# A third scatter accumulator in a mixture-of-experts block: rotated, loaded early, and summed half on VectorE and half in PSUM

## The reference, cut to what matters

```python
x = x + conv(layernorm_over_channels(x), W)       # W: product of 32 reflections, 128 x 128
t = tokens(x)                                     # 4096 tokens of 128 channels, float32
h = softmax(layernorm(t) @ W_router + b_router)   # 32 experts
G, idx = top_k(h.T, 128)                          # each expert picks 128 tokens
up = silu(tokens[idx] @ W_up + b_up)              # 128 -> 341
eo = G * (up @ W_down + b_down)                   # 341 -> 128
y = zeros(4096, 128).at[idx].add(eo)              # a token may be picked by several experts
out = t + y                                       # back to NCHW
```

## Time and profile before

| | us |
|---|---|
| median of 3 runs | 192.45 (191.24 to 192.54) |
| the profiled execution | 192.84 |
| its span, first to last instruction | 191.0 |
| busy: PE, POOL, DVE, ACT | 130.8, 110.7, 83.3, 80.6 |

### The profile page before, as it was taken

How to read it: one execution, slowest core, us unless ns; L and a number is a source line. 1 busy time by engine, 2 the same in 40 slices (tenths; PEclk the granted TensorE clock), 3 DMA queues, 4 the chain that set the end, 5 groups by cost and what they waited for, 6 DMA issues and landing times.

```text
span 191.0 us, 2379 instructions
## 1 busy us (share of the span) xinstructions
PE 130.8 (68%) x670; PEld 86.7 (45%) x673; DVE 83.3 (44%) x374; ACT 80.6 (42%) x290; POOL 110.7 (58%) x119
## 2 busy tenths in 40 slices
PE   0999983432421644479999999998399999500892
PEld 0556972321101412247666787668234444200892
DVE  1464898985578489800112222128912200000550
ACT  3167799554798277854553335540000000000162
POOL 2017658998632037777777788775878878730000
PEclk9999999995555555555999999999969999975588
DMA  4999999999956243222222233341332333378987
GB/s 89 299 329 319 289 294 228 226 407 293 247 169 195 81 184 105 72 69 69 63 63 66 69 44 28 31 40 14 29 28 27 31 33 36 27 160 304 389 261 234
DMA packets 33662, 28.37 MB, mean 149 GB/s; under 512 B 6832, under 2 KB 27376, under 8 KB 33520
## 3 DMA queue, kind: packets, MB, share of 16 engines
q1 hardware_dynamic: 26785, 21.70, 39.0%
q0 software_dynamic: 5424, 4.39, 15.9%
q10 hardware_dynamic: 1440, 2.13, 3.4%
HBM read 17.53 MB, written 10.68 MB: 148 GB/s over the span
## 4 chain that ended last, share of the span: by engine, by line
PE 38%; POOL 20%; DVE 14%; DMA 12%; issue 11%; ACT 4%; SPq 0%; POOLq 0%
POOL acc L503 7%; PE PT L1128 7%; PE PZ L1142 7%; DMA acc<-X,idx 6%; PE PM L1128 6%; POOL rs L464 4%; DMA x<-acc 3%; PE PM L1142 3%; PE PZ L1169 3%; POOL rs L457 3%; PE PT L975 3%; POOL act L470 2%; DMA k<-in_const_f 2%; PE PT L1117 2%; DVE junk L913 2%
## 5 line engine op out<-in xcount | busy, mean ns | idle before, releaser
L503 POOL DMA_INDIRECT acc<-X,idx x27 | 45.6, 1690 | 13.5 <-issue 8.2
L494 POOL DMA_INDIRECT xg<-token_rows,idx x32 | 30.6, 955 | 20.4 <-DVE idx L910 11.9
L632 ACT ACTIVATE X<-PZ 128x512 f32<-128x512 f32 x4 | 2.4, 597 | 52.6 <-PE PZ L1169 52.6
L951 DVE TENSOR_SCALAR X<-PZ,xg 128x128 f32<-128x128 f32 x22 | 7.6, 349 | 27.9 <-PE PZ L1142 27.9
L1023 PE MATMUL PZ<-stage_w,X 128*128 128x192 f32 x64 | 14.7, 382 | 6.9 <-DVE act L754 6.5
L1142 PE MATMUL PZ<-wdn,act 128*128 128x128 f32 x132 | 17.6, 280 | 0.5 <-DVE X L951 0.5
L959 DVE TENSOR_TENSOR x<-x,xf 128x512 f32<-128x512 f32 x8 | 5.4, 692 | 28.2 <-DMA x<-acc 28.2
L1142 PEld LDWEIGHTS PZ<-wdn,act 128*128 128x128 f32 x132 | 16.4, 196 | 1.3 <-DVE X L951 0.7
L1023 PEld LDWEIGHTS PZ<-stage_w,X 128*128 128x128 f32 x64 | 12.5, 226 | 8.3 <-DVE act L754 7.5
L1128 PE MATMUL PT<-xgT,wup 128*128 128x512 f32 (+3 forms) x28 | 15.0, 620 | 2.0 <-ACT xgT L616 2.0
L625 ACT ACTIVATE act<-PT,bup 128x512 f32<-128x512 f32 (+3 forms) x14 | 9.0, 640 | 14.5 <-PE PT L1128 14.5
(11 more groups left out here) (177 smaller groups left out, 276.0 us busy)
## 6 DMA issues: line engine op xcount, KB each, us to landing
X<-in_x SPq DMA_DIRECT2D x8, 256.0 KB, 5.3
acc<-zero SPq DMA_DIRECT2D x4, 512.0 KB, 6.4
acc<-x SPq DMA_DIRECT2D x8, 256.0 KB, 5.6
token_rows<-xf SPq DMA_DIRECT2D x8, 256.0 KB, 2.3
xf<-acc ACTq DMA_DIRECT2D x8, 256.0 KB, 6.9
x<-acc SPq DMA_DIRECT2D x8, 256.0 KB, 8.5
out<-X SPq DMA_DIRECT2D x8, 256.0 KB, 2.5
wup<-in_L_ffn_W_up SPq DMA_DIRECT2D x1, 1364.0 KB, 7.7
```

What stands on the lines that cost most here:

```text
L494: nc.gpsimd.indirect_dma_start(out=xg[:, e, :], out_offset=None, in_=rows[:, :], in_offset=bass.IndirectOffsetOnAxis(ap=idx[:, e:e + 1], a ...
L503: nc.gpsimd.indirect_dma_start(out=acc[i][:, :], out_offset=bass.IndirectOffsetOnAxis(ap=idx[:, e:e + 1], axis=0), in_=eo[:, e, :], in_off ...
```

## The change

A third accumulator, acc2, is filled with zeros after the token rows were stored. The scatters of experts 0 to 17 go to acc0, acc1 and acc2 in turn, those of 18 to 26 to acc0 and acc1 alternately. acc2 is therefore complete after expert 17 and is loaded to SBUF (y2, over xg, which is free once all expert outputs are scaled) from ScalarE's queue: two chunks after each of the scatters of experts 18, 19, 20 and 21 has landed. VectorE adds y2 to y1 in place, and PE goes twice over the eight banks: first with y1 + y2, then with y0.

```diff
@@ -66,7 +66,8 @@
 SCATTERED = E - ON_PE
 HOTS = 3
 
-INTO = tuple((SCATTERED - 1 - e) % 2 for e in range(SCATTERED))
+ROTATED = SCATTERED // 3 * 2
+INTO = tuple(e % 3 if e < ROTATED else (SCATTERED - 1 - e) % 2 for e in range(SCATTERED))
 AHEAD = E
 
 
@@ -117,7 +118,7 @@
     ALU, ACT, AX = mybir.AluOpType, mybir.ActivationFunctionType, mybir.AxisListType
 
     rows = nc.dram_tensor("token_rows", (TOK, ROW), f32, kind="Internal").ap()
-    acc = [nc.dram_tensor(f"acc{i}", (TOK, C), f32, kind="Internal").ap() for i in range(2)]
+    acc = [nc.dram_tensor(f"acc{i}", (TOK, C), f32, kind="Internal").ap() for i in range(3)]
 
     ctx = ExitStack()
     with ctx:
@@ -247,7 +248,8 @@
         lg = act[:, 0, :, :].rearrange("p j n -> p (j n)")[:, 0:CH * P].rearrange("p (g u e) -> p g u e", g=CH, u=TPC)
         pr = act[:, 1, :, :].rearrange("p j n -> p (j n)")[:, 0:CH * P].rearrange("p (g u e) -> p g u e", g=CH, u=TPC)
 
-        y0, y1, ysum, yo = x1, xf, x1, X
+        y0, y1, yo = x1, xf, X
+        y2 = xg[:, :, :].rearrange("p e c -> p (e c)")[:, 0:TOK].rearrange("p (t c) -> p t c", c=C)
         columns = wide16[:, :, :].rearrange("p i n -> p (i n)")
 
 
@@ -332,6 +334,7 @@
         s_rows_s = sem("rows_s_stored")
         s_acc0 = sem("acc0_filled")
         s_acc1 = sem("acc1_filled")
+        s_acc2 = sem("acc2_filled")
         s_sum = sem("count_sums_ready")
         s_tie = sem("tie_totals_ready")
         s_tieb = sem("tie_bases_ready")
@@ -356,9 +359,11 @@
         s_part = sem("expert_out_parts_ready")
         s_hot = sem("token_onehot_ready")
         s_hotu = sem("token_onehot_used")
-        s_sc = [sem(f"scattered{i}") for i in range(2)]
-        s_y = [sem(f"y_loaded{g}") for g in range(CH)]
-        s_ys = sem("y_summed")
+        s_sc = [sem(f"scattered{i}") for i in range(3)]
+        s_y0 = [sem(f"y0_loaded{g}") for g in range(CH)]
+        s_y1 = [sem(f"y1_loaded{g}") for g in range(CH)]
+        s_y2 = [sem(f"y2_loaded{g}") for g in range(CH)]
+        s_ys = sem("y1_y2_summed")
         s_yT = sem("y_transposed")
         s_yo = sem("y_out_ready")
         s_out = sem("out_stored")
@@ -422,12 +427,14 @@
                 else:
                     sp.wait_ge(s_xfp, CH - g)
                 sp.dma_start(rows_v[g, :, :, 0:C], per_chunk(xf, g)).then_inc(s_rows_x, 16)
+            for q in range(4):
+                sp.dma_start(acc[2][q * 1024:(q + 1) * 1024, :].rearrange("(p k) c -> p (k c)", p=P), zero[:, :]).then_inc(s_acc2, 16)
 
             sp.wait_ge(s_idx, 1)
             sp.dma_start(columns, ccol.to_broadcast([P, TOK])).then_inc(s_col, 16)
             sp.wait_ge(s_sc[0], 16 * INTO.count(0))
             for g in range(CH):
-                sp.dma_start(per_chunk(y0, g), acc_v[0][g]).then_inc(s_y[g], 16)
+                sp.dma_start(per_chunk(y0, g), acc_v[0][g]).then_inc(s_y0[g], 16)
             for g in range(CH):
                 sp.wait_ge(s_yo, g + 1)
                 sp.dma_start(out_v[g // 2, g % 2], yo[:, g, :].rearrange("p (u n) -> p u n", u=TPC)).then_inc(s_out, 16)
@@ -498,8 +505,10 @@
             def scatter(e):
                 pool.wait_ge(s_eo, e + 1)
                 i = INTO[e]
-                if e >= 2:
+                if INTO[:e].count(i):
                     pool.wait_ge(s_sc[i], 16 * INTO[:e].count(i))
+                elif i == 2:
+                    pool.wait_ge(s_acc2, 16 * 4)
                 nc.gpsimd.indirect_dma_start(
                     out=acc[i][:, :], out_offset=bass.IndirectOffsetOnAxis(ap=idx[:, e:e + 1], axis=0),
                     in_=eo[:, e, :], in_offset=None, compute_op=ALU.add).then_inc(s_sc[i], 16)
@@ -624,9 +633,16 @@
                     src = PT[0:fn, 1, 0:n * P] if (3 * k + j) % 2 == 0 else PM[0:fn, 0, 0:n * P]
                     nc.scalar.activation(act[0:fn, k % 2, j, 0:n * P], src, ACT.Silu, bias=bup[0:fn, j, e0 // PER:e0 // PER + 1]).then_inc(s_act, 1)
             a.wait_ge(s_rows_x, 16 * CH)
+            a.wait_ge(s_eo, E)
+            a.wait_ge(s_sc[2], 16 * INTO.count(2))
+            for g in range(CH):
+                if g % 2 == 0:
+                    e = ROTATED + g // 2
+                    a.wait_ge(s_sc[INTO[e]], 16 * INTO[:e + 1].count(INTO[e]))
+                a.dma_start(per_chunk(y2, g), acc_v[2][g]).then_inc(s_y2[g], 16)
             a.wait_ge(s_sc[1], 16 * INTO.count(1))
             for g in range(CH):
-                a.dma_start(per_chunk(y1, g), acc_v[1][g]).then_inc(s_y[g], 16)
+                a.dma_start(per_chunk(y1, g), acc_v[1][g]).then_inc(s_y1[g], 16)
             for g in range(CH):
                 a.wait_ge(s_yT, g + 1)
                 nc.scalar.activation(yo[:, g, :], out_bank(g), ACT.Copy).then_inc(s_yo, 1)
@@ -945,6 +961,7 @@
                 if e == SCATTERED + ON_PE // 2:
                     v.wait_ge(s_rows_s, 16 * CH)
                     v.wait_ge(s_acc1, 16 * 4)
+                    v.wait_ge(s_acc2, 16 * 4)
                     v.wait_ge(s_eo, e)
                     split(0, ON_PE // 2)
                 v.wait_ge(s_dn, e + 1)
@@ -955,8 +972,9 @@
                 token_onehot(k)
 
             for g in range(CH):
-                v.wait_ge(s_y[g], 32)
-                nc.vector.tensor_tensor(per_chunk(ysum, g), per_chunk(y0, g), per_chunk(y1, g), ALU.add).then_inc(s_ys, 1)
+                v.wait_ge(s_y2[g], 16)
+                v.wait_ge(s_y1[g], 16)
+                nc.vector.tensor_tensor(per_chunk(y1, g), per_chunk(y1, g), per_chunk(y2, g), ALU.add).then_inc(s_ys, 1)
 
         @block.tensor
         def _(pe):
@@ -1166,7 +1184,11 @@
             for g in range(CH):
                 pe.wait_ge(s_ys, g + 1)
                 for u in range(TPC):
-                    ins = mm(out_bank(g)[:, u * P:(u + 1) * P], ysum[:, g * TPC + u, :], ident, start=False, stop=(u == TPC - 1))
+                    mm(out_bank(g)[:, u * P:(u + 1) * P], y1[:, g * TPC + u, :], ident, start=False, stop=False)
+            for g in range(CH):
+                pe.wait_ge(s_y0[g], 16)
+                for u in range(TPC):
+                    ins = mm(out_bank(g)[:, u * P:(u + 1) * P], y0[:, g * TPC + u, :], ident, start=False, stop=(u == TPC - 1))
                 ins.then_inc(s_yT, 1)
```

## The result

Twenty runs of each kernel: median 193.02 us (191.96 to 195.12) with the change, 192.1 us (188.49 to 193.48) before, a step of 0.9 us or 0.5%. The means of all twenty, 193.17 and 191.91, differ by 0.7%. So the change is slower, by 0.5 to 0.8%. Forecast were 192.8 us in a range of 190.4 to 195.5, 0.3 us above the kernel before, with 0.57 for a step within 1% and 0.29 for slower.

A forecast was written before the change was run, and what follows sets the result against it. Two stretches were taken to set the end: POOL's scatters and a 20.4 us tail behind their last landing. Scatters -2.6 us and tail +2.9 gave +0.3, so 192.8 us, in a range of 190.4 to 195.5.

The forecast's parts named there:

- The waits of e0 to e19: POOL's scatters: with three accumulators the waits go, 3.89 us gained over scatters 0 to 17, 4.2 by scatter 20.
- VectorE beside POOL: One-hots beside scatters 0 to 17: the 3.1 us of longer scatters stays, plus 0.4 us of new collisions.
- Rival F: Three one-hots at 130.46 to 134.64 take POOL for their whole 3.8 us: 194.6 us; chance 0.04.
- The loads beside the alternating scatters: Third accumulator's loads beside scatters 20 to 26: +0.8 us per landing, counted for scatters 20 and 22.
- rival D: Loads hold back three scatters by 1.4 us each and more, 4.2 in place of 1.6: 195.4 us; chance 0.13.
- The tail: From the last scatters' landings through loads and PE's two passes: second pass cannot start earlier, costing 2.9 us.
- E: PE's second pass starts at half clock and takes 9.87 us in place of 7.16: 195.5 us; chance 0.07.
- C: Loads hardly disturb scatters, and the second accumulator's loads get more than their share: 190.7 or 190.3 us; chance 0.14.
- The sum: Whole kernel: -2.6 us for the scatters' end and +2.9 for the tail, +0.3 in all, 192.8 us.
- What was priced at nothing: Third accumulator's fill at 62 to about 69 us and the new waits on it: zero; gathers not delayed.

The follow-up runs named there:

- e18: Not a run: POOL's scatter 18, counted from 0, first of those alternating between two accumulators in the change; started at 150.10 us in the kernel before.
- e20: Not a run: POOL's scatter 20, counted from 0; landed after 5.63 us in the changed kernel, 3.3 before.
- e10: Not a run: POOL's scatter 10, counted from 0, beside VectorE's one-hots; grew by 0.55 us in the kernel before.
- e11: Not a run: POOL's scatter 11, counted from 0, beside VectorE's one-hots; took 2.66 us in the kernel before.
- e17: Not a run: POOL's scatter 17, counted from 0, the last that uses three accumulators in turn in the changed kernel.
- e22: Not a run: POOL's scatter 22, counted from 0; landed after 5.80 us in the changed kernel, 3.2 before.
- e24: Not a run: POOL's scatter 24, counted from 0; waits for e22, with a gap of 2.67 us before it in the changed kernel.
- e26: Not a run: the last of POOL's 27 scatters, counted from 0; started at 167.05 us in the kernel before and landed after 3.51.
- before_light: Kernel before, with PE multiplying only one of three bfloat16 parts in the one-hot product: 191.84 us, ratio 0.996 to the kernel before.
- after_light: Changed kernel, with PE multiplying only one of three bfloat16 parts in the one-hot product: 193.41 us, ratio 1.008 to the kernel before.
- mixed4_light: As after_light, but only chunks 0 to 3 go twice over PE and VectorE adds the first accumulator for 4 to 7: 191.01 us, ratio 0.994.
- not_loaded_light: As after_light, but without the eight loads of the third accumulator: 189.34 us, ratio 0.988 to the kernel before.
- e23: Not a run: POOL's scatter 23, counted from 0, one of those alternating between two accumulators; landing forecast near 4.1 us.

## Why the prediction was right, and where it was not

**The waits of e0 to e19 went, by the price forecast.** e18 was to come 36.8 us after e0 and came after 36.33; e20 after 41.1, it was 40.29. From e1 to e19 no gap is above 0.31.

**VectorE beside POOL was sized right.** 0.55 + 1.11 + 0.4 = 2.06 us for e10 and e11; the rows above give 0.77 + 1.30 = 2.07. Over e0 to e17 the scatters grew by 2.9 us in all, where 3.1 + 0.4 were forecast; that is most of the 0.5 us by which e18 came early. The Trainium skill's rule of an exclusive hold (SBUF — State Buffer, "Who interferes with whom") would have given 3.8. The trace agrees that there is a collision, but POOL loses about half of the one-hots' length. Rival F is out.

**The loads beside the alternating scatters are where the prediction failed.** The step had the mechanism, the place and the number of scatters on the chain right: e20 and e22, after which the loads are through. Its size was wrong. From e20 to e22 it takes 6.36 us and from e22 to e24 6.54, where four were normal: 2.4 and 2.5 us per landing in place of 0.8, so 4.9 in place of 1.6. It was rival D's mechanism at more than D's price, and it had been given 0.13. Two readings led there. First, e26 of the earlier trace rows was taken as a lower bound because loads ran beside its second half; it landed in 3.5 us then, with the first load issued 1.44 us after its start. With 1.32 us (after) and 1.3 (before_light, after_light) it took 4.6 us, with 1.2 (mixed4_light, not_loaded_light) 4.9. So that row stood on an edge and said nothing of a full overlap. Second, +0.8 was taken as the middle between that row and two others, and not from the engines' time, although the prediction had this right: 7 us for the loads, 0.75 for each scatter, "the engines are full" (its 1.7 us for a pair of loads is 1.8 at its own 286 GB/s). From e20's start to e22's landing, 149.12 to 161.28, the queues show:

```profile
q10 hardware_dynamic: 1145, 2.09, 53.9%
q0 software_dynamic: 706, 0.32, 31.9%
```

That is 6.6 us of all engines for the loads and 3.9 for the scatters, 10.4 us, in a stretch that took 7.3 us before. An estimate from these: if loads and scatters share the engines without either having precedence, the stretch grows by some 3.2 us, where 1.6 was forecast; it grew by 4.9. The other 1.7 are not accounted for. The Trainium skill (DMA: Bandwidth & Descriptors, "Latency and other measured facts") has an HBM latency of up to 2 us at high load, 0.2 on average. Landings of +1.9, +2.3, +0.8, +2.5 and +1.4 us for e19 to e23 are of that size, three of them above the 1.8 us that lie between the page's two figures. Whether the growth is waiting for an engine or latency is not shown by any run here: both would go away with the loads.

**The tail was right in kind and 0.9 us too dear.** PE's second pass took 7.16 us at full clock, without a gap, as forecast (E is out). From the first load of the second accumulator to PE's end 21.9 us were forecast and 21.05 measured. The term at fault is the last load of the second accumulator, 13.1 us after the first issue. It landed after 10.4 (at 170.8 + 6.9), since the loads of the first accumulator came 3.25 us behind it and not 2.1: the 4.6 us landing of e26 held them back. PE, from 171.52, was then never short of data, the case that C described for the first pass (chance 0.14), though not for C's reason. What the second pass costs is thus 2.0 us against the kernel before here, and 6.7 where PE sets the end.

**The sum** was -2.6 + 2.9 = +0.3 us, and the traces give, from e0 to PE's end, -0.1 - 0.1 + 2.0 = +1.8: scatters, the gap from e26 to the first load, tail. Within the scatters' -0.1 the landings were 3.3 us dearer than forecast and the stretch up to e20 0.8 us better. That the span grew by only 0.9 is the 0.98 us by which e0 came earlier in this trace, which no part of the change explains; in the four light kernels e0 starts anywhere from 108.94 to 109.55. The prediction's total was near partly by luck: the scatters were mis-sized by 2.5 us the one way, the tail by 0.9 the other, and the front came 1 us early. The sum gave a step of 0.3 us; the medians moved by 0.9.

**What was priced at nothing** stayed so: the gathers began at the same distance before e0, their longest landing was 3.9 us against 4.0, and the new waits on the fill met no one.

## What to carry to other kernels

Traffic hidden beside a chain of small transfers, each of which waits for one before it, is not hidden: multiply the growth of one landing by the number of links beside it, and take as its lower bound that small transfers and loads share the engines' time; where the chain has slack (three accumulators, 5.55 us against 4.03) the same load should cost less, which was not run. When a sum is moved from VectorE to an accumulating pass on TensorE, the pass that waits for the last input is what the end pays; give it few chunks (four here, 2.4 us better than eight) and let VectorE sum the rest. And a neighbour row that overlaps only at its edge is no bound for full overlap.

## What the runs showed of the hardware that was not expected

- A scatter of 128 rows of 512 bytes that adds to DRAM lands in 3.2 to 3.4 us alone and in 5.3 to 5.8 us beside 512 KB of loads (e20 and e22 of the changed kernel, after_light and mixed4_light). The DMA engines are busy for 0.81 to 0.91 of that time in the changed kernel. Spreading the same bytes over twice as many scatters hardly helped (16.90 against 17.28 us from e20 to e26).
- A low share of the DMA engines within a transfer does not show that they had time to spare: in the kernel before it is 0.00 from 160 to 161 us, while e22 is under way undisturbed, and of e20 in the changed kernel nine of 144 packets moved only between 154.0 and 154.5, after 1.1 us in which loads alone moved.
- On two of the three chips of the experiments, VectorE and ScalarE stood for up to 5.2 us at a time without a visible reason while POOL issued its gathers, PE reached the down product some 24 us later, and both kernels ran 12 to 19 us longer. A change can cost 0.5 to 0.8% on one chip and 3.3% on the next because another engine sets the end.
